# First attention layer of a graph network: sums with the attention weights stationary, the rows moving

## The reference, cut to what matters

```python
h = (x @ W).reshape(N, H, C)                       # H = 4, C = 512
e = leaky_relu(al_s[src] + al_d[dst], 0.2)
m = segment_max(e, dst); ex = exp(e - m[dst])
denom = segment_sum(ex, dst)
out = segment_sum(h[src] * (ex / (denom[dst] + 1e-16)), dst) + b1
h = elu(out)                                       # goes on into h @ W2
```

## Time and profile before

| | |
|---|---|
| three runs, median | 1367.67 us |
| profiled execution | 1367.73 us |
| its span, first to last instruction | 1365.9 us |
| mean granted clock of TensorE | 0.961 of full |
| front, and h for all heads | 0 to 331 us |
| first attention layer, main loop | 331 to 919 us |
| second attention layer | 926 to 1060 us |
| convolutions | 1060 to 1366 us |

### The profile page before, as it was taken

The page is one execution under the profiler, slowest core; times in us unless marked ns, Lnnn a source line. Parts: engine busy times, 40 slices in busy tenths (PEclk is TensorE's granted clock), DMA queues, the critical chain, the costliest instruction groups (busy, mean ns, idle before and its releaser), DMA issues. The chain is left out here.

```text
span 1365.9 us, 21543 instructions
## 1 busy us (share of the span) xinstructions
PE 1210.9 (89%) x7822; PEld 1125.2 (82%) x7822; DVE 939.4 (69%) x1935; ACT 520.8 (38%) x1169; POOL 49.2 (4%) x42
## 2 busy tenths in 40 slices
PE   2799898998988997899898999985999699979998
PEld 2676686687887997799898999974999699979998
DVE  7788888885686777868787867887785843354322
ACT  1323131315554655456553755415542511132210
POOL 7000000001000000000000000000000500000000
PEclk9999999999999999999999999996999899999999
DMA  5020212100100201010100210003000300041010
GB/s 184 16 98 36 70 72 93 40 1 24 47 0 1 78 11 37 1 57 22 47 1 14 65 47 0 1 1 112 14 0 1 116 36 36 24 157 48 24 36 33
DMA packets 29899, 58.08 MB, mean 43 GB/s; under 512 B 4882, under 2 KB 10042, under 8 KB 29792
## 3 DMA queue, kind: packets, MB, share of 16 engines
q1 hardware_dynamic: 29600, 56.31, 12.5%
q10 hardware_dynamic: 192, 0.32, 0.1%
HBM read 41.08 MB, written 15.54 MB: 41 GB/s over the span
## 5 line engine op out<-in xcount | busy, mean ns | idle before, releaser
L1158 PE MATMUL banks<-ring_hi,hs 128*128 128x256 f32 (+1 forms) x1600 | 325.2, 287 | 7.7 <-DVE ring_lo L472 4.4
L1158 PEld LDWEIGHTS banks<-ring_hi,hs 128*128 128x128 f32 x1600 | 267.7, 195 | 10.3 <-issue 5.4
L1158 PE MATMUL banks<-ring_lo,hs 128*128 128x256 f32 (+1 forms) x800 | 228.0, 285 | 0.0
L1648 PE MATMUL p_y<-cr_hi,g_hi 128*128 128x256 f32 (+1 forms) x600 | 147.4, 288 | 19.6 <-ACT cr_hi L1507 14.4
L1158 PEld LDWEIGHTS banks<-ring_lo,hs 128*128 128x128 f32 x800 | 156.1, 195 | 0.0
L446 ACT ACTIVATE e<-banks,al 128x256 f32<-128x256 f32 (+1 forms) x400 | 153.0, 488 | 7.7 <-PE banks L431 7.7
L454 ACT ACTIVATE ring_hi<-pf 128x512 fp32r<-128x512 f32 (+1 forms) x125 | 80.3, 643 | 186.9 <-DVE pf L465 167.6
L1648 PE MATMUL p_y<-cr_hi,g_lo 128*128 128x256 f32 (+1 forms) x600 | 146.5, 286 | 0.0
L1186 PE MATMUL banks<-w_hi,oT_hi 128*128 128x384 f32 (+1 forms) x320 | 112.3, 351 | 27.2 <-DVE rows L923 23.2
L1648 PEld LDWEIGHTS p_y<-cr_hi,g_hi 128*128 128x128 f32 x600 | 118.2, 197 | 21.3 <-ACT cr_hi L1507 19.3
L1648 PEld LDWEIGHTS p_y<-cr_hi,g_lo 128*128 128x128 f32 x600 | 118.3, 197 | 0.0
(11 more groups left out here) (219 smaller groups left out, 2344.7 us busy)
## 6 DMA issues: line engine op xcount, KB each, us to landing
h_scratch<-stage SPq DMA_DIRECT2D x30, 256.0 KB, 2.0
hs<-h_scratch SPq DMA_DIRECT2D x30, 256.0 KB, 2.9
w_st<-in_L_gnn_W SPq DMA_DIRECT2D x4, 1536.0 KB, 10.1
w_st<-in_L_gnn_W SPq DMA_DIRECT2D x16, 384.0 KB, 3.4
gw_st<-in_L_gnn_W SPq DMA_DIRECT2D x12, 384.0 KB, 3.2
xr<-in_x SPq DMA_DIRECT2D x9, 384.0 KB, 6.6
rows<-in_x SPq DMA_DIRECT2D x9, 384.0 KB, 3.5
g_scratch<-orow SPq DMA_DIRECT2D x18, 192.0 KB
```

What stands on the lines that cost most here:

```text
L1158: nc.tensor.matmul(p_a[:, f, 0:n], hs[:, s, a, cols], r, start=s == 0 and j == 0, stop=s == T - 1 and j == 2)
L1648: last = nc.tensor.matmul(p_y[:, f, 0:n], hs[a][:, s, f * P:(f + 1) * P], c_hi[:, i % RS, s % G, 0:n], start=s + a == 0, stop=s == T - 1 a ...
```

## The change

The operands of the sums change places. The ring's weights, 128 sources by 128 destinations, are now stationary, and the rows h move, 516 columns in two halves of 258: 512 features, two columns of ones (the first gives the denominator), two of zeros. Destinations are on partitions now, so `normalize` is a reciprocal of one column for each 128 destinations and one operation that multiplies by it and adds b1, which is spread over partitions by four DMAs. relu and exp have no bias any more and run in 4 operations of 512 columns. The products need features on partitions, so z is turned: `turn_out`, 4 transposes for 128 destinations, stands in the sums of the next chunk after source tiles 3 and 6 and goes through one bank, from which ScalarE takes the hi part and VectorE the lo part before the second turn.

Order changes with it. On VectorE `elu_lo` goes in two pieces to the next round, behind the first and second group; the maxima go between the adds, spread 2, 3, 3, 2 over chunks 0 to 3; the first two W2 splits stand ahead of the fifth group. On TensorE the last two turns of `turn_next` go from source tiles 5 and 8 to 7 and 9, and in the last ten tiles of h the turns of `top0`, of its shifts and the first broadcast come 2 to 3 tiles earlier, the degrees later.

The diff, cut to its core:

```diff
+HA = HID + 4
+HH = HA // 2
+TURNS = (3, 6)
...
-    p_a = banks[:, 2:6, :]
-    p_den = banks[:, 6, :]
+    p_a = banks[:, 2:6, :].rearrange("p (t b) c -> p t b c", b=2)
+    p_o = banks[:, 6, :].rearrange("p (f c) -> p f c", f=KH)
...
-            sp.dma_start(bcol[:, :], b1.rearrange("(f p) -> p f", p=P), allow_slow_non_contiguous=True).then_inc(b_in, 16)
...
+                sp.dma_start(b1bc[:, h, 0:HID], b1.rearrange("(a n) -> a n", a=HEADS)[h:h + 1, :].to_broadcast([P, HID])).then_inc(b_in, 16)
...
+            pool_.wait_ge(rows_done, 1)
+            pool_.wait_ge(wlo_done, HEADS * KD)
+            nc.gpsimd.memset(hs[:, :, 0, HID:HID + 2].bitcast(fp32), 1.0).then_inc(ones_done, 1)
+            nc.gpsimd.memset(hs[:, :, 0, HID + 2:HA].bitcast(fp32), 0.0).then_inc(ones_done, 1)
+            nc.gpsimd.memset(hs[:, :, 1, HID:HA].bitcast(fp32), 0.0).then_inc(ones_done, 1)
...
-                h, n = q // NC, CHUNKS[q % NC][1]
-                if q == 0:
-                    act.wait_ge(b_in, 16)
                 act.wait_ge(z_done, q + 2)
-                for f in range(KH):
-                    b = bcol[:, h * KH + f:h * KH + f + 1]
-                    nc.scalar.activation(pos[:, f, 0:n], z[:, f, 0:n], ACT.Relu, bias=b)
-                    last = nc.scalar.activation(ev[:, f, 0:n], z[:, f, 0:n], ACT.Exp, bias=b)
+                for dts, m in tile_groups(q):
+                    for dt in range(NDT)[dts]:
+                        nc.scalar.activation(pos[0:m, dt, :], z[0:m, dt, 0:HID], ACT.Relu)
+                        last = nc.scalar.activation(ev[0:m, dt, :], z[0:m, dt, 0:HID], ACT.Exp)
                 last.then_inc(exp_done, 1)
 
-            def elu_hi(q):
-                n = CHUNKS[q % NC][1]
-                act.wait_ge(o_done, q + 1)
-                nc.scalar.activation(oT[0][:, :, 0:n], z[:, :, 0:n], ACT.Copy, bias=-1.0).then_inc(ohi_done, 1)
+            def elu_hi(q, dt):
+                m = rows_of(q % NC * NDT + dt)
+                act.wait_ge(turned, q * NDT + dt + 1)
+                nc.scalar.activation(oT[0][:, :, dt * P:dt * P + m], p_o[:, :, 0:m], ACT.Copy, bias=-1.0).then_inc(ohi_done, 1)
...
+                    last, second_last = before(q, 1), before(q, 2)
                     for g in range(NG):
                         wt.exps(nc, act, scores, q, c, g)
-                        if q == 0 and g == 0:
-                            row_hi(T - 1)
+                        if second_last is not None and g == 0:
+                            elu_hi(second_last, 0)
+                        if q == 0 and g <= 1:
+                            row_hi(T - 2 + g)
                         if g >= 1:
                             wt.hi(nc, act, q, c, g - 1)
+                        if second_last is not None and g == 1:
+                            elu_hi(second_last, 1)
...
+                    if c == 1:
+                        split_weights(h, range(2))
...
-            dve.wait_ge(deg_done, 1)
-            nc.vector.tensor_copy(deg[:, :], p_d).then_inc(deg_done, 1)
-            for t in range(4, 7):
-                row_lo(t)
+            row_lo(4)
             dve.wait_ge(top_t, 1)
             nc.vector.tensor_reduce(mem.amax[:, :], p_top0[:, 0:T, :], AX.X, ALU.max).then_inc(reduced, 1)
             shift_parts(nc, chain, mem, 0, lambda: dve.wait_ge(reduced, 1), shift_ready)
-            row_lo(7)
+            row_lo(5)
             dve.wait_ge(shift_t, 1)
             nc.vector.tensor_copy(shiftT[:, 0, :], p_s0).then_inc(shift_out, 1)
-            row_lo(8)
+            row_lo(6)
+            row_lo(7)
...
+                h, first = q // NC, q % NC * NDT
                 dve.wait_ge(wt.used, (q + 2) * NG)
-                nc.vector.reciprocal(rden[:, 0:n], p_den[:, 0:n]).then_inc(rden_done, 1)
-                dve.wait_ge(rden_done, q + 1)
-                for f in range(KH):
-                    last = nc.vector.tensor_tensor(z[:, f, 0:n], p_a[:, f, 0:n], rden[:, 0:n], ALU.mult)
+                for dt in range(NDT):
+                    m = rows_of(first + dt)
+                    nc.vector.reciprocal(rden[0:m, dt:dt + 1], p_a[0:m, dt, 1, HID - HH:HID - HH + 1]).then_inc(rden_done, 1)
+                if q == 0:
+                    dve.wait_ge(b_in, 16 * HEADS)
+                    dve.wait_ge(ones_done, 4)
+                for dt in range(NDT):
+                    m = rows_of(first + dt)
+                    dve.wait_ge(rden_done, q * NDT + dt + 1)
+                    last = nc.vector.scalar_tensor_tensor(out=z[0:m, dt, :].rearrange("p (b c) -> p b c", b=2), in0=p_a[0:m, dt, :, 0:HH],
+                                                          scalar=rden[0:m, dt:dt + 1],
+                                                          in1=b1bc[0:m, h, :].rearrange("p (b c) -> p b c", b=2),
+                                                          op0=ALU.mult, op1=ALU.add)
                 last.then_inc(z_done, 1)
 
             def elu_out(q):
-                n = CHUNKS[q % NC][1]
                 dve.wait_ge(exp_done, q + 1)
-                nc.vector.scalar_tensor_tensor(out=z[:, :, 0:n], in0=ev[:, :, 0:n], scalar=1.0, in1=pos[:, :, 0:n],
-                                               op0=ALU.min, op1=ALU.add).then_inc(o_done, 1)
-
-            def elu_lo(q):
-                n = CHUNKS[q % NC][1]
-                dve.wait_ge(ohi_done, q + 1)
-                nc.vector.scalar_tensor_tensor(out=oT[1][:, :, 0:n], in0=z[:, :, 0:n], scalar=-1.0,
-                                               in1=oT[0][:, :, 0:n].bitcast(fp32), op0=ALU.add, op1=ALU.subtract)\
+                for dts, m in tile_groups(q):
+                    last = nc.vector.scalar_tensor_tensor(out=z[0:m, dts, 0:HID], in0=ev[0:m, dts, :], scalar=1.0, in1=pos[0:m, dts, :],
+                                                          op0=ALU.min, op1=ALU.add)
+                last.then_inc(o_done, 1)
...
+            def elu_lo(q, dt):
+                m = rows_of(q % NC * NDT + dt)
+                dve.wait_ge(ohi_done, q * NDT + dt + 1)
+                nc.vector.scalar_tensor_tensor(out=oT[1][:, :, dt * P:dt * P + m], in0=p_o[:, :, 0:m], scalar=-1.0,
+                                               in1=oT[0][:, :, dt * P:dt * P + m].bitcast(fp32), op0=ALU.add, op1=ALU.subtract)\
                     .then_inc(olo_done, 1)
...
+            def next_top(h, c, part):
+
+                first = (0, 1, 2, 3, 5, 6, 8, 9, T, T, T)
+                for t in range(first[2 * c + part], first[2 * c + part + 1]):
...
+                        if second_last is not None and g == 0:
+                            elu_lo(second_last, 0)
                         if q == 0 and g == 0:
-                            row_lo(T - 1)
+                            row_lo(T - 2)
+                            dve.wait_ge(deg_done, 1)
+                            nc.vector.tensor_copy(deg[:, :], p_d).then_inc(deg_done, 1)
                         if g >= 1:
                             wt.lo(nc, dve, q, c, g - 1)
+                        if second_last is not None and g == 1:
+                            elu_lo(second_last, 1)
...
+                    if not final:
+                        next_top(h, c, 0)
                     if second_last is not None:
-                        add_products(second_last, range(2, NB))
+                        add_products(second_last, range(2, 3))
+                    if not final:
+                        next_top(h, c, 1)
+                    if second_last is not None:
+                        add_products(second_last, range(3, NB))
                     if c == 0:
                         split_rows(h, 3)
+                    if c == 1:
+                        split_weights(h, range(2))
...
-                    if last is not None:
-                        elu_lo(last)
                     if c == 1:
-                        split_weights(h)
-                    if c < NC - 1 and not final:
-                        next_top(h, c)
...
-            between = {0: score_columns, 3: degrees, 6: turn_top, 7: lambda: turn_shift(0, p_s0), 8: spread_first}
+            between = {0: score_columns, 4: turn_top, 5: lambda: turn_shift(0, p_s0), 6: spread_first, 7: degrees}
...
-                if s == 5:
...
+                if s == 7:
...
-                if s == 8:
+                if s == 9:
                     turn_shift(h + 1, p_g[1][0:4 * T, 0:P])
+
+            def turn_out(q, dt):
+                m = rows_of(q % NC * NDT + dt)
+                pe.wait_ge(o_done, q + 1)
+                pe.wait_ge(olo_done, q * NDT + dt)
+                for f in range(KH):
+                    last = nc.tensor.transpose(p_o[:, f, 0:m], z[0:m, dt, f * P:(f + 1) * P], ident[0:m, 0:m])
+                last.then_inc(turned, 1)
...
-                    hi, lo = (wt.ring[a][:, s // G, s % G, 0:n] for a in range(2))
-                    for f in range(KH):
-                        cols = slice(f * P, (f + 1) * P)
```

(18 more changed lines are left out.)

69 lines of the change are left out of this document (37 added, 32 removed).

## The result

The changed kernel takes 1314.51 us, the median of 4 runs (1309.19 to 1319.27), against 1368.75 us of the kernel before on the same chip: a ratio of 0.9605, 95% interval 0.9565 to 0.9646. On a second chip it was 1312.77 against 1369.13, ratio 0.9600 (0.9575 to 0.9626). The forecast was 1312 us, in a range from 1283 to 1346. The profiled execution took 1315.24 us with a span of 1313.7.

The account below looks back on a forecast made before the run. TensorE, busy 89% of the span, was taken as the bound. Savings of 20.4 us work, 33.2 waits and half pace, and 2.6 at the start, less 0.4 behind the last products, took 1367.7 to 1312 us, range 1283 to 1346.

Parts of the forecast that it names:

- z of the first chunk: Head 0: TensorE waits 1.9 us for z of its first chunk, where it waited 3.3 before.
- first turn of head 0: Three maxima and two splits stand ahead of `elu_out` with no products to hide them: 3.3 us and some 2 of half pace.
- first turns in chunk 1: One more maximum and two weight splits delay `elu_out`: some 1.0 us of wait at the first turn.
- turn of maxima at tile 7: Chunk 3: the turn of the last two maxima waits 1.2 us for the reduce behind `elu_lo`.
- keep_shift: After chunk 3's sums, the next products wait 2.0 us for `keep_shift`, which comes three groups on.
- chunks 0: First chunk of a head: two pairs of row splits ahead of normalize make the first add 2.5 us late.
- last head: Scores and maxima stand ahead of the last `elu_lo` in the last head: 2.7 us of wait.
- the end: End of the last head: turn, copy and lo, twice, cost 2.6 us of wait and 2.0 of half pace.
- A: Rival: the waits only move; waits and half pace stay at 72 us, only work and start gain: 1345 us; chance 0.17.
- B: Rival: nearly no waits, the walk being pessimistic; 10 us left for 39: 1283 us; chance 0.14.
- C: Rival: the turns bring the clock down, 2.0 us of half-pace loss in each of 20 chunks: 1352 us; chance 0.05.
- D: Rival: slower, TensorE waits at both turns in each chunk, 5.5 us a chunk: 1416 us; chance 0.04.

Follow-up runs that it names:

- light0: Changed kernel with one pair of chunk 0's row splits moved behind normalize on VectorE, and chunk 0's maxima in heads 1 and 2 moved earlier: 1310.31 us, ratio 0.9574.
- light0_both: Changed kernel with chunk 0 relieved of maxima and one pair of row splits on VectorE, and ScalarE's copies of those rows behind the exps: 1307.81 us, ratio 0.9549.
- best2: Changed kernel with shifts turned in another bank, maxima and reduces re-placed, last-head elu_lo earlier, chunk 0's first three row-split pairs later on both engines: 1292.42 us, ratio 0.9446.
- order_only: Kernel before with its old sums and no turns of z, only the new places of maxima and W2 splits: 1318.54 us, ratio 0.9634; again 1318.34 us, 0.9630.
- form_only: Changed kernel with maxima and W2 splits put back where the kernel before had them: 1357.06 us, ratio 0.9906.
- turns_twice: Changed kernel with each turn's four transposes issued twice into the same bank, 160 transposes more: 1328.06 us, ratio 0.9692.

## Why the prediction was right, point by point

**TensorE's work.** Predicted 38.4 us less for the sums and 18 more for the turns, 20.4 in all. Measured by the same count: a chunk is 120 x 0.1232 = 14.78 us of sums (14.64), 0.71 of two turns (0.9), 8.47 of products (8.33 before). 20 x 23.96 is 479.2, with 11.2 for broadcasts and 3 x 1.4 for turns of maxima 494.6 us. Against the 513.2 of before (its turns of maxima at the same price) that is 18.6 less; against the prediction's 515.3 it is 20.7. The turns of z were cheaper than put, sums and products dearer. The prediction's upper bound for the turns, 0.25 us each, was the whole duration of a group of 8 (1.97 us); from start to start it was 1.62, 0.20 each.

**Losses.** Predicted 72.5 down to 39.3, 33.2 less; measured 587.8 - 513.2 = 74.6 down to 536.7 - 494.6 = 42.1, 32.5 less. Place by place: z of the first chunk 1.8 (1.9); the first turn of head 0 2.6 (3.3); first turns in chunk 1 1.3 in heads 1 and 2 (1.0) and none in the last; turn of maxima at tile 7 1.15 (1.2); `keep_shift` 1.5 (2.0); chunks 0 1.83 (2.5); last head 3.0 (2.7); the end 1.5, 1.2 and 1.4 (2.6); and 1.4 at the first broadcast, which the prediction did not have. The waits inside the layer add up to 29.3 us where the prediction's terms hold 33.3, and six stretches of 3.4 us at half clock cost up to 10.2 where it put 6; 2.6 us are not assigned. So the sum is nearer than its parts: waits put too high and half pace put too low offset each other, and that much of the hit is luck.

**Start and end.** Predicted 2.6 less, measured 1.5; the wait for the first `ring_lo` fell from 4.4 to 2.1, as said. But the order-alone kernel, which touches nothing ahead of the layer, started it 2.8 us earlier too, so the start itself varies by as much as this term. Behind the layer 0.5 (0.4).

**What was off: the cause of one wait.** The step "two pairs ahead of normalize make it late by 4.3, the first add comes 2.5 us late" names VectorE's row splits in chunk 0. light0 took one pair away and the wait went from 1.83 to 1.71 only; light0_both moved ScalarE's copy too and it fell to 0.68. The size was near because both engines are late by nearly the same (450.71 with VectorE's splits, 450.62 when it waits for ScalarE), and the walk had followed only one. The wait is set by whichever of two engines is later, and either one's block makes it; ScalarE's block moved alone was not tried.

**What the sum hid: the terms are not separate gains.** I booked 20 us to the work and 33 to the waits. The runs say: order alone 0.963, form alone 0.991, both 0.960. The layer of each, from the windows of its profile, split by the counts above:

| kernel | layer us | work | losses |
|---|---|---|---|
| before | 587.8 | 513.2 | 74.6 |
| order alone | 537.0 | 513.2 | 23.8 |
| form alone | 579.3 | 494.6 | 84.7 |
| both (the change) | 536.7 | 494.6 | 42.1 |
| both, waits mended (best2) | 515.7 | 494.6 | 21.1 |

The rows are of one profiled execution each; in a second one of each the layer took 534.3 us for the change and 539.1 for the order alone, so differences of 2 to 3 us between two rows are within what one kernel varies by.

The order takes 51 us of losses from the old form, where I expected some 35. The form takes 18.6 us of work and brings 18.3 of losses in the new order, 10 in the old. So in the shipped pair the form earns almost nothing: 0.960 against 0.963, with intervals (0.9575 to 0.9626, and 0.9612 to 0.9647) that overlap, so that even this rest is not clear of noise. My expectation for order_only took the waits of the changed kernel for those of the order. They were those of the form: the two turns tie TensorE to VectorE and ScalarE twice more in a chunk, and the reduces and `keep_shift` came to stand where a bank was needed. best2 removes most of them and gets some 20 us back. Whether its moves would also speed up the old form was not tried: with the order alone that form has 23.8 us of losses left, so it could gain something too.

**The rivals.** A (losses stay at 72) fell for the pair, but is what form_only shows. B (10 us of losses) fell: the change keeps 42.1, even best2 21.1. C fell with turns_twice. D's waits at the turns exist, six in the change (10.0 us) and more in form_only, and nowhere in plain chunks.

**Still open.** Why half pace follows one wait and not the next is not settled. Here are the 3.33 us behind the same wait of the changed kernel, in the round of chunk 0 of head 1, in the first of its two profiled executions and then in the second:

```profile
454.77:458.10 3.33, 3.33 (x11) 3.33 (x12) 2.41 (x4) 2.75 (x6) 0.00 (x0) 0.51 0.00 0
```

```profile
452.14:455.47 3.33, 3.33 (x19) 3.33 (x20) 3.32 (x6) 2.75 (x6) 0.00 (x0) 1.00 0.00 0
```

Both had waited 1.83 us for the same add, ending at 454.77 and 452.14; the third number from the right is the granted clock, 0.51 and 1.00. The first execution had six stretches of half clock in the layer, the second four. The reverse happened at the end of the layer, behind waits of 1.50 and 1.19 us in a row, again first and second execution:

```profile
855.95:859.28 3.33, 3.33 (x19) 3.33 (x20) 3.12 (x7) 0.00 (x0) 0.00 (x0) 1.00 0.00 0
```

```profile
851.60:854.93 3.33, 3.33 (x10) 3.33 (x11) 3.12 (x7) 0.00 (x0) 0.00 (x0) 0.50 0.00 0
```

No run told apart what decides it.

## What to carry to other kernels

Move the long blocks of a helper engine into the gaps where it waits for the bound engine before changing the form of the work: here that alone was nine tenths of the gain, and the new form gave next to nothing until its own waits were mended. When a wait is put down to one engine, walk every engine in its loop: if two are late by about the same, relieving one changes next to nothing. A round trip added to the bound engine costs its waits in chunks where the helpers are full, not on average; count slack there.

## What the runs showed of the hardware

- A 128x128 transpose of fp32 on TensorE costs 0.09 us in a group of four (0.35 us for four, the switches in it), and each of four more that follow adds 0.109, at full clock; after 8 of them in each turn the sums of plain chunks kept their full pace.
- In the kernel before every stretch at half clock in this layer stands behind an idle of 3.3 us or more. In the changed kernel it was also seen behind idles of 1.8 to 3 us, behind two of 2.13 and 1.36 us that ended 4.5 us apart (at 329.71 and 334.20 us; granted clock 0.63 from there to 338.80), and behind two of 1.50 and 1.19 us in a row (granted clock 0.50), in some executions and not in others. A single idle of 0.99 us between products was never followed by it, neither before nor with the order alone.
- The matmuls with 258 columns moving run 0.123 us apart, those with 256 ran 0.1195, 3.7 ns more, 0.04 us over the 12 of a source tile, and two matmuls of 0.12 each are gone. How much of the 3.7 ns is the two columns and how much the exchange of the operands was not told apart.
